# Rebuilding the opening of a graph and LSTM kernel: bias, item parts, late weights and the first layer norm

## The reference

```
x = x + relu(adj @ (item_feat @ W_item.T + b_item) + layernorm(x) @ W_user.T + b_user)
h = lstm(layernorm(x))                       # 10000 steps, 128 wide
g = argmax(h @ W_lin.T + b_lin)              # 0 or 1 for each step
w = g * h;  inc = cumsum(w)
x = x + 2 h + (inc - w) * fw_att + (inc[-1] - inc) * bw_att
```

## Time and profile before

| what | us |
|---|---|
| median of 3 runs | 1538.49 (1537.8 to 1540.41) |
| the profiled execution's own time | 1538.81 |
| its span, first to last instruction | 1537.0 |
| mean granted clock of TensorE, as a share of 2.4 GHz | 0.985 |
| first matmul | 8.04 |
| first adjacency matmul | 19.89 |
| end of the block stage | 1199.9 |
| busy in the span: PE / DVE / ACT / POOL | 1471.3 / 1201.8 / 1083.2 / 193.2 |

### The profile page before, as it was taken

The page is one execution under the profiler, slowest core; times in us unless marked ns, Lnnn a source line. Parts: engine busy times, 40 slices in busy tenths (PEclk is TensorE's granted clock), DMA queues, the critical chain, the costliest instruction groups (busy, mean ns, idle before and its releaser), DMA issues.

```text
span 1537.0 us, 25512 instructions
## 1 busy us (share of the span) xinstructions
PE 1471.3 (96%) x7890; PEld 1251.9 (81%) x7890; DVE 1201.8 (78%) x2018; ACT 1083.2 (70%) x1581; POOL 193.2 (13%) x172
## 2 busy tenths in 40 slices
PE   6999999999999999999999999999999899999991
PEld 5887887887887887887887887787787799999991
DVE  5998888888888888888888887887887456566667
ACT  4677777777777777777777777777776455556661
POOL 0000000000000000000000000000000000046765
PEclk9999999999999999999999999999999899999996
DMA  9789999999999999999999999999997300000003
GB/s 373 274 307 371 353 345 371 353 343 371 353 344 371 351 346 371 353 344 370 352 346 370 353 343 362 354 341 369 353 346 277 141 0 0 0 1 0 0 0 134
DMA packets 70080, 426.73 MB, mean 278 GB/s; under 512 B 8674, under 2 KB 17698, under 8 KB 69540
## 3 DMA queue, kind: packets, MB, share of 16 engines
q1 hardware_dynamic: 68320, 425.12, 73.1%
q10 hardware_dynamic: 1732, 1.24, 0.3%
HBM read 416.09 MB, written 10.24 MB: 277 GB/s over the span
## 4 chain that ended last, share of the span: by engine, by line
issue 77%; PE 20%; DVE 1%; POOL 0%; ACT 0%; POOLq 0%; DVEq 0%
PE psZ L729 9%; PE psZ L739 9%; PE psZ L745 1%; DVE y L1146 1%; POOL rstd L381 0%; POOLq L384 0%; DVE cum L1069 0%; ACT normed L492 0%; DVE cum L1067 0%; PE psV L639 0%; DVE dif L1057 0%; DVE dif L1054 0%; ACT u L506 0%; DVE y L1140 0%; DVE dif L1059 0%
## 5 line engine op out<-in xcount | busy, mean ns | idle before, releaser
L863 DVE TENSOR_TENSOR a_lo<-raw,a_hi 128x1000 fp32r<-128x1000 f32 (+1 forms) x800 | 907.4, 1180 | 139.6 <-ACT a_hi L521 136.1
L521 ACT ACTIVATE a_hi<-raw 128x1000 fp32r<-128x1000 f32 (+1 forms) x800 | 803.9, 1029 | 204.3 <-PE psG L664 185.6
L662 PE MATMUL psG<-a_hi,item_hi 128*128 128x500 f32 (+1 forms) x1580 | 637.0, 403 | 17.5 <-DVE a_lo L863 17.4
L664 PE MATMUL psG<-a_hi,item_lo 128*128 128x500 f32 (+1 forms) x1580 | 616.5, 390 | 0.0
L663 PE MATMUL psG<-a_lo,item_hi 128*128 128x500 f32 (+1 forms) x1580 | 613.6, 388 | 0.0
L662 PEld LDWEIGHTS psG<-a_hi,item_hi 128*128 128x128 f32 (+1 forms) x1580 | 297.0, 188 | 98.6 <-DVE a_lo L863 28.8
L664 PEld LDWEIGHTS psG<-a_hi,item_lo 128*128 128x128 f32 (+1 forms) x1580 | 298.1, 189 | 61.4
L663 PEld LDWEIGHTS psG<-a_lo,item_hi 128*128 128x128 f32 (+1 forms) x1580 | 298.0, 189 | 61.1 <-issue 4.4
L381 POOL TENSOR_TENSOR rstd<-var,minus_half 125x4 f32<-125x4 f32 x40 | 74.3, 1859 | 1119.4 <-DVE var L847 1119.4
L729 PE MATMUL psZ<-u,wx 128*128 (+1 forms) x1280 | 158.0, 277 | 1.6 <-POOL u L389 1.6
L729 PEld LDWEIGHTS psZ<-u,wx 128*128 128x128 f32 x1280 | 154.4, 194 | 3.6 <-issue 2.0
(11 more groups left out here) (111 smaller groups left out, 575.9 us busy)
## 6 DMA issues: line engine op xcount, KB each, us to landing
raw<-in_adj_main SPq DMA_DIRECT2D x360, 1000.0 KB, 5.7
raw<-in_adj_main SPq DMA_DIRECT2D x40, 750.0 KB, 4.1
x_copy<-xb SPq DMA_DIRECT2D x20, 250.0 KB, 5.2
x<-x_copy SPq DMA_DIRECT2D x1, 5000.0 KB, 15.5
out<-y SPq DMA_DIRECT2D x25, 200.0 KB, 2.4
xb<-in_xT SPq DMA_DIRECT2D x18, 250.0 KB, 5.4
u<-in_itemT SPq DMA_DIRECT2D x3, 1024.0 KB, 18.7
u<-in_itemT SPq DMA_DIRECT2D x1, 904.0 KB, 24.0
```

What stands on the lines that cost most here:

```text
L521: nc.scalar.activation(a_hi[:, s % CUT, 0:n], raw[:, r % RAW, at:at + n], ACT.Copy)\
L662: pe.matmul(bank, w_hi, hi, start=(c == 0), stop=False)
L664: last = pe.matmul(bank, w_lo, hi, start=False, stop=(c == CH))
L863: dve.tensor_tensor(a_lo[:, s % CUT, 0:n], raw[:, r % RAW, at:at + n], a_hi[:, s % CUT, 0:n].bitcast(f32), ALU.subtract).then_inc(lo_ready, 1)
```

## The change

- **Bias by a matmul.** The spreading transfer of b_item goes. One row of 128 values is loaded into `bi_row` (a new tile of one partition, set between item_hi and item_lo), a matmul with ones spreads it into the bank psW, and DVE copies it to `bi`. PE's first quad waits only for W_item beyond this.
- **Item parts in turn with pieces.** Quads 0 / 1-2 / 3-4 / 5-6 / ... / 15-16 / 17-19 are ten transfers. SP issues quad 0, piece 0, quads 1-2, piece 1, quads 3-4, and so on; after piece r comes part r + 1, up to r = 8.
- **Late weights for later.** Of the 14 transfers of ACT five stay ahead: W_item, bi_row, block 0 of x, W_user, b_user. The other nine are issued after the halves of pieces 0 to 9 in ACT's list (`late_loads`; W_lin, b_lin, fw and bw behind pieces 6, 7, 8 and 9). W_user and b_user have a semaphore of their own. Behind the five stands an activation of one element, which waits for the constants.
- **First layer norm during the pieces.** PE's to_rows stands after piece 0; DVE's stats, pair_up and eps after piece 1, row_scale after piece 2; ACT's normalise after piece 3; PE's to_columns after piece 4; ACT's out_v after piece 5; the bias matmul of block 0 after piece 7 (it was after piece 2).

```diff
-PARTS = (0, 1, 4, 8, 12, 16, QUADS)
+PARTS = (0, 1, 3, 5, 7, 9, 11, 13, 15, 17, QUADS)
+FIRST = dict(rows=0, stats=1, scale=2, norm=3, back=4, out=5, bias=7)
+        bi_row = sb("bi_row", [1, HID], f32, first)
...
             load_items(0)
-            load_items(1)
-            load_block(0, wait=False, move=False, items={0: (2,), 2: (3,), 3: (4, 5)})
+            load_block(0, wait=False, move=False, items={r: (r + 1,) for r in range(len(PARTS) - 2)})
...
             act.dma_start(wi[:, :], w_itemT).then_inc(wi_in, 16)
-            act.dma_start(bi[:, :], b_item[0:1, :].to_broadcast([P, HID])).then_inc(wi_in, 16)
+            act.dma_start(bi_row[:, :], b_item[0:1, :]).then_inc(bi_in, 16)
             act.dma_start(xb[:, 0, :], xT[:, cols(0)]).then_inc(x_in[0], 16)
-            act.dma_start(wx[:, :], w_ihT).then_inc(wx_in, 16)
-            act.dma_start(bb[0:1, :], b_ih).then_inc(wx_in, 16)
-            act.dma_start(bb[1:2, :], b_hh).then_inc(wx_in, 16)
-            act.dma_start(wu[:, :], w_userT).then_inc(w_in, 16)
-            act.dma_start(bu[:, :], b_user).then_inc(w_in, 16)
-            act.dma_start(wh[:, :], w_hhT).then_inc(w_in, 16)
...
-            act.dma_start(xb[:, 1, :], xT[:, cols(1)]).then_inc(x_in[1], 16)
+            act.dma_start(wu[:, :], w_userT).then_inc(wu_in, 16)
+            act.dma_start(bu[:, :], b_user).then_inc(wu_in, 16)
+
+            act.wait_ge(const_ready, 7)
+            nc.scalar.activation(normed[0:1, 0:1], ones[0:1, 0:1], ACT.Copy)
+
+            def late_loads(r):
+                if r == 0:
+                    act.dma_start(wx[:, :], w_ihT).then_inc(wx_in, 16)
+                if r == 1:
+                    act.dma_start(bb[0:1, :], b_ih).then_inc(wx_in, 16)
+                    act.dma_start(bb[1:2, :], b_hh).then_inc(wx_in, 16)
+                if r == 2:
+                    act.dma_start(xb[:, 1, :], xT[:, cols(1)]).then_inc(x_in[1], 16)
+                if r == 4:
+                    act.dma_start(wh[:, :], w_hhT).then_inc(w_in, 16)
+                if r == 6:
+                    act.dma_start(wl[:, :], w_linT).then_inc(w_in, 16)
...
+                if r == 9:
+                    act.dma_start(bwc[:, :], bw).then_inc(w_in, 16)
...
# ACT, in body, after both halves and the item part of piece r:
-                    if items and r == 1:
+                    if items:
+                        late_loads(r)
+                    if items and r == FIRST["norm"]:
+                        normalise(0)
+                    if items and r == FIRST["out"]:
                         out_v(0)
...
             item_hi_part(0)
-            normalise(0)
...
# PE, in body, after the matmuls of piece r:
-                    if items and r == 0:
+                    if items and r == FIRST["rows"]:
+                        pe.wait_ge(x_in[0], 16)
+                        to_rows(0, 0)
+                    if items and r == FIRST["back"]:
                         to_columns(0)
-                    if items and r == AT["bias"]:
-                        pe.wait_ge(w_in, 16 * 7)
-                    if r == AT["bias"]:
+                    if items and r == FIRST["bias"]:
+                        pe.wait_ge(wu_in, 32)
+                    if r == (FIRST if items else AT)["bias"]:
...
             pe.wait_ge(const_ready, 7)
+            pe.wait_ge(bi_in, 16)
+            pe.matmul(psW[:, 0:HID], ones[0:1, :], bi_row[:, :], start=True, stop=True).then_inc(bi_psum, 1)
             item_quad(0)
             item_quad(1)
-            pe.wait_ge(x_in[0], 16)
-            to_rows(0, 0)
             item_quad(2)
...
# DVE, in body, after the second half and the item part of piece r:
+                    if items and r == FIRST["stats"]:
+                        stats(0)
+                        pair_up(0)
+                        eps(0)
+                    if items and r == FIRST["scale"]:
+                        row_scale(0)
...
-            dve.wait_ge(wi_in, 32)
-            dve.wait_ge(const_ready, 7)
+            dve.wait_ge(bi_psum, 1)
+            dve.tensor_copy(bi[:, :], psW[:, 0:HID]).then_inc(bi_ready, 1)
+            dve.wait_ge(bi_ready, 1)
             item_sum_part(0)
             item_sum_part(1)
             item_lo_part(0)
-            stats(0)
-            pair_up(0)
-            eps(0)
-            row_scale(0)
             body(0, has2=False, items=True)
...
-            dve.wait_ge(w_in, 16 * 7)
+            dve.wait_ge(w_in, 16 * 5)
```

More of the change, by code:

```diff
@@ L189, in program @@
         wi_in = sem("wi_in")
+        bi_in = sem("bi_in")
+        bi_psum = sem("bi_psum")
+        bi_ready = sem("bi_ready")
+        wu_in = sem("wu_in")
         w_in = sem("w_in")
@@ L468, in _ @@
             act.dma_start(wi[:, :], w_itemT).then_inc(wi_in, 16)
-            act.dma_start(bi[:, :], b_item[0:1, :].to_broadcast([P, HID])).then_inc(wi_in, 16)
+            act.dma_start(bi_row[:, :], b_item[0:1, :]).then_inc(bi_in, 16)
             act.dma_start(xb[:, 0, :], xT[:, cols(0)]).then_inc(x_in[0], 16)
-            act.dma_start(wx[:, :], w_ihT).then_inc(wx_in, 16)
-            act.dma_start(bb[0:1, :], b_ih).then_inc(wx_in, 16)
-            act.dma_start(bb[1:2, :], b_hh).then_inc(wx_in, 16)
-            act.dma_start(wu[:, :], w_userT).then_inc(w_in, 16)
-            act.dma_start(bu[:, :], b_user).then_inc(w_in, 16)
-            act.dma_start(wh[:, :], w_hhT).then_inc(w_in, 16)
[L477 to L480, removed]
-            act.dma_start(xb[:, 1, :], xT[:, cols(1)]).then_inc(x_in[1], 16)
+            act.dma_start(wu[:, :], w_userT).then_inc(wu_in, 16)
[14 more added lines that the diff above has]
+                    act.dma_start(wl[:, :], w_linT).then_inc(w_in, 16)
+                if r == 7:
+                    act.dma_start(bl[:, :], b_lin[0:1, :].to_broadcast([P, 2])).then_inc(w_in, 16)
+                if r == 8:
+                    act.dma_start(fwc[:, :], fw).then_inc(w_in, 16)
+                if r == 9:
+                    act.dma_start(bwc[:, :], bw).then_inc(w_in, 16)
             def relu(j):
@@ L694, in item_quad @@
                 if q == 0:
-                    pe.wait_ge(wi_in, 32)
+                    pe.wait_ge(wi_in, 16)
                 if q in PARTS:
```

## The result

The changed kernel takes 1531.92 us (median of 6 runs, 1530.1 to 1532.95), the kernel before 1538.14 (6 runs, 1537.36 to 1540.41). The ratio is 0.9957, with a 95% interval of 0.9945 to 0.9969: 6.2 us shorter. The forecast was 1531.7.

A forecast was written before the change was run, and what follows sets the result against it. PE was taken to bound the kernel from 38 us to 1199.9, leaving the opening to gain from: -5.9 - 1.3 - 0.5 + 0.45 + 0.4 = -6.85, so 1531.7 us with the runs' median 0.3 below the profile; range 1529.5 to 1536.0.

The forecast's parts named there:

- Piece 0 at 14.0 instead of 19.89, -5.9: Opening: PE's first adjacency matmul starts 5.9 us earlier, at 14.0 (12.8 to 16.4), behind quad 3.
- The broadcast slows the transfers: Opening, 4 to 7 us: b_item's broadcast holds all transfers to 210 GB/s; without it, over 350 GB/s.
- Half clock, -1.3 of at most -1.9: Piece 0 on PE: 1.9 us was put to the clock; 0.6 lost after the change, a gain of 1.3.
- Full clock by 16: Sign to look for in the opening: PE's clock at its full level by 16 us.
- The bias matmul's wait, -0.5: Block 0 on PE: the bias matmul no longer waits for bw and its weights, 0.5 us gained.
- to_rows in block 0, +0.45: Block 0 on PE: four transpositions of the first layer norm come in, adding 0.45 us.
- DVE's part of the norm, +0.4 (0 to 1.6): Block 0's first pieces: moments and small instructions on DVE, without lead yet, add 0.4 us (0 to 1.6).
- ACT's issues: Block 0: nine late transfer issues on ACT, at most 0.70 us each but for the slow one, cost nothing.
- the slower rival with 2.2 us an issue: Pieces 0 to 9: long late issues hold ACT, 1539 to 1541 us; decides from 2.2 us an issue; chance 0.05.
- Does the stream keep up?: Block 0: transfers stay ahead of PE up to piece 8, which lands at 39.5, by 3 us at the narrowest.
- No wait for raw longer than 1 us: Sign to look for in block 0: no wait for raw above 1 us between pieces 1 and 9.
- What comes behind is unchanged: Blocks 1 to 19, LSTM and output: unchanged, starting 6.85 us earlier; the stage's end near 1193.

The follow-up runs named there:

- a1_broadcast: Changed kernel with b_item again spread over 128 partitions by the transfer, without bias matmul and copy: 1532.17 us, 0.9964 of the kernel before.
- b3_norm_and_order: Kernel before with only the first layer norm moved into the pieces and item parts in turn with pieces: 1531.27 us, 0.9952 of the kernel before.
- a4_loads_front: Changed kernel with the nine late loads back at the head of ACT's list, behind the five: 1531.91 us, 0.9959 of the kernel before.
- second profile: Changed kernel run again unaltered, beside two kernels with added matmuls: 1531.21 us, 0.9952 of the kernel before.
- c1_warm: Changed kernel with 16 matmuls of 128 columns added in PE's idle stretches ahead of piece 0: 1531.67 us; run again, 1529.90 us.
- c2_warm_quad3: Changed kernel with matmuls added in PE's idle stretches, only two behind quad 2, and quad 3 in the second item part: 1530.00 us; again, 1530.77 us.
- b1_norm_only: Kernel before with only the first layer norm moved into the pieces: 1538.91 us, 1.0004 of the kernel before.
- a3_old_parts: Changed kernel with item parts cut and transfers ordered as before: 1537.54 us, 0.9994 of the kernel before.

## Why the prediction was right

- *Piece 0 at 14.0 instead of 19.89, -5.9.* 14.61 in one profile and 14.12 in the other, so -5.3 to -5.8. The third part was taken to land at 12.9, and quad 3 began at 12.89 and 13.20, as it landed. Quad 3 released piece 0, as forecast; the first a_lo (from 11.59, done at 12.8) was not late. From quad 3's start to piece 0 were 1.7 and 0.9 us.
- *The broadcast slows the transfers.* Right: 207 to 236 GB/s between 4 and 7 us in the five traces that have it, 402 to 428 in the others. bi_row landed by 3.75 and 4.04, not at or after 4.05 with 2 us on top, and quad 0 began at 4.44 and 4.74, earlier than my 5 to 6.5. I let this carry the choice of 12.9 against 14.5. With the broadcast (a1_broadcast, b3_norm_and_order) quad 3 was released at 14.14 and 14.59, and the medians show no loss. By the profiles at full pace there is one of 1.8 to 1.9 us at the end of block 0; the changed kernel's first execution lost as much to its clock, so that these two ended block 0 where it did. A later start does not by itself find full pace: a4_loads_front came at 15.07 and had half, a1_broadcast at 15.06 and had full.
- *Half clock, -1.3 of at most -1.9.* Piece 0 took 18.71 - 14.61 = 4.1 us where 2.8 is full pace: 1.3 lost, a gain of 0.6; in the second profile nothing was lost, a gain of 1.9. My -1.3 lies midway between two cases of which I could only say that I could not tell them apart; that it fits the two on average is luck. "Full clock by 16" held in the second profile (from 13.2) and failed in the first, where it came at 17.3 to 17.6. The working also misread the old opening: full pace came there within quads 2 and 3 (16 matmuls in 2.64 us from 12.44), 5 to 6 us after the first matmul and not 7.
- *The bias matmul's wait, -0.5.* From the quad ahead of it to the next are 45.68 - 41.21 = 4.47 us, for 3.60 + 0.85; before they were 33.62 - 28.66 = 4.96. Right.
- *to_rows in block 0, +0.45.* 19.15 - 18.71 = 0.44.
- *DVE's part of the norm, +0.4 (0 to 1.6).* 0 in both profiles of the changed kernel; 0.8 and 0.5 in a1_broadcast and b3_norm_and_order, where PE came at full pace to a late start, 0.25 in c1_warm, 0.8 in c2_warm_quad3. It is inside the range, but the 0.4 in the sum was not there.
- *ACT's issues.* Nothing, as costed; the slower rival with 2.2 us an issue fell at 0.26 to 0.38. My reason against it, that the slow one followed thirteen unfinished transfers, does not hold: in a4_loads_front 14 issues stand in a row too, with b_item as one row, and the last took 0.49 us. It took 1.40 to 2.42 in the four traces that have 14 with the broadcast among them; why is open.
- *Does the stream keep up?* Yes, in both profiles no wait for raw reached PE. Piece 8 was forecast for 39.5 and was waited for until 40.2. "No wait for raw longer than 1 us" was wrong: in the first profile at piece 9 with 1.52 us, in the second at pieces 3, 7, 8 and 9 with 1.23 to 1.57. And the cover was thinner than the 3 us that I had: in the second profile piece 7 was waited for until 37.56, its a_lo was done at 39.8, and PE took it up at 40.2.
- *What comes behind is unchanged.* Stage end at 1193.2, forecast near 1193.

The sum was -6.85, and the runs have -6.2. That they lie so close is in part luck. In the first profile the terms come to -6.0 (-5.3 for the start, -0.6 for the clock, -0.5, +0.45, and nothing for DVE), and only the later blocks' waits make it -6.7 at the stage's end; in the second they come to -7.8. The terms on the start, the bias wait and to_rows were right by their mechanism; the one on the clock was a mean of two cases. (The low end of my own range, -8.9, does not follow from its terms: they give -8.65 with the 0.4 for DVE and -9.05 without.) What the prediction did not see is how the parts hang together. It put the gain to the start and named the stream as a check on the side. The runs show two conditions of equal weight: the norm out of the chain brings the early start (b1_norm_only), and only the item parts in turn keep it, since the early start turns the old order's lateness at piece 4, which was hidden in the kernel before, into 4 us of idleness and up to 2 more of half clock (a3_old_parts, b1_norm_only).

What stays open: what decides whether the clock stands at its full level at piece 0 of the changed kernel, and how often it does; two profiles had one each way. Two smaller questions stay with it: how much of the 1.8 us that the bias part shows in the profiles comes through in the time, and whether filling PE's gaps brings full pace every time; it did in four of four profiles. The Trainium skill (TensorE: Matmul & The Clock Gate, "Part 1: The HAM clock gate") says that the number of slow matmuls at a kernel's start varies from run to run, with the phase that the activity monitor has at the start. The two profiles of the changed kernel agree that it varies; the phase is in no trace here.

## What to carry to other kernels

When a chain at the start of a kernel is cut short, look at what its length had hidden: go through the transfers in the order of their queue and compare each landing with the new time of need, not the old one. Queue the first work's data, then only as much of the next as the next piece needs. A part of a change that measures as nothing alone may be the half without which the other half is worth nothing, so test parts in pairs before dropping one.

## What the hardware showed that I had not expected

- One transfer that spreads a row of 512 B over 128 partitions, 64 KB in all, holds the transfers of all queues together at about half their rate for 3 to 4 us, until it lands near 8 us: 207 to 236 GB/s between 4 and 7 us in the five traces that have it, 402 to 428 in the nine that don't.
- In the first 17 us the granted clock in the windows reads 1.00 even where PE's matmuls run at half pace (eight of 128 columns in 2.07 us, later 1.05; in the changed kernel's first profile 0.62 us a matmul of 500 columns between 15 and 17, later 0.39). The pace there has to be read from the durations.
- The same program came to piece 0 at half pace in one execution and at full pace in another, with the same gaps ahead of it to within 0.4 us.
